# A four-layer graph network on one core: low and high parts split from PSUM, row sums on TensorE, and an earlier start of the masked layer's loads

## The reference, cut to what matters

```python
h = relu(layernorm(x)); x = x + (1 - 0.1 * h - 0.01 * sum(h * (adj @ h), axis=1))          # layer 0
for k in range(2): h = tanh(concat([adj @ h, h]) @ W[k])                                  # layer 1, two hops
mask = (adj != 0); rank = cumsum(mask, axis=1); k = min(deg, 100); pos = rank - (deg - k)
w = mask * where(pos > 0, 0.5 ** (k - pos), 0);  x = x + w @ (h @ weight) + bias           # layer 2, masked
x = x + (tanh(concat([h, t]) @ W1 + b1) @ W2 + b2) + adj @ (h @ B.T) - rowsum(adj) * (h @ B.T)   # layer 3
```

## Time and profile before

| | us |
|---|---|
| median of 3 runs | 698.91 |
| profiled execution, its own time | 700.7 |
| its span, first to last instruction | 698.9 |
| TensorE matmuls busy | 668.3 |
| VectorE busy | 469.6 |
| ScalarE busy | 192.5 |
| GpSimd busy | 114.2 |

### The profile page before, as it was taken

One profiled execution on the slowest core, in us unless ns is written; L12 is line 12 of the kernel. 1 busy time (PEld: TensorE's weight loads), 2 busy tenths in 40 slices (PEclk: granted clock), 3 DMA queues, 4 the chain that ended last, 5 costly groups with the idle time before them and its releaser, 6 DMA issues.

```text
span 698.9 us, 10418 instructions
## 1 busy us (share of the span) xinstructions
PE 668.3 (96%) x3811; PEld 270.2 (39%) x3824; DVE 469.6 (67%) x813; ACT 192.5 (28%) x296; POOL 114.2 (16%) x132
## 2 busy tenths in 40 slices
PE   3999999999999999999999998899999999999997
PEld 1434433334433333333344443444444443333332
DVE  7777767777899999996888888899989810000000
ACT  1101111011111001101111116899998811111111
POOL 4110011110200000001222223222332211211111
PEclk9999999999999999999999999999999999999999
DMA  8999999998589999959999983999999479999992
GB/s 347 422 410 411 413 412 409 418 414 335 190 329 388 420 422 419 415 206 402 384 406 420 419 368 134 362 378 408 414 414 412 191 263 341 417 415 418 417 419 98
DMA packets 42098, 256.51 MB, mean 367 GB/s; under 512 B 5120, under 2 KB 11264, under 8 KB 11840
## 3 DMA queue, kind: packets, MB, share of 16 engines
q1 hardware_dynamic: 38712, 252.85, 89.6%
q10 hardware_dynamic: 3336, 3.00, 1.5%
HBM read 252.28 MB, written 3.54 MB: 366 GB/s over the span
## 4 chain that ended last, share of the span: by engine, by line
PE 53%; DMA 20%; DVE 19%; POOL 4%; issue 3%; ACT 0%; SPq 0%; DVEq 0%; ACTq 0%; POOLq 0%
PE accA L1373 37%; DMA cache<-adj_blocks 10%; DVE uS L1111 8%; DMA land<-adj_blocks 6%; PE accA L1424 4%; PE work L1408 4%; DVE uS L1155 3%; POOL rstd L762 2%; DMA rows_transposed<-rowsT 2%; PE work L1391 1%; PE work L1336 1%; POOL tS L772 1%; PE accA L1342 1%; PE work L1267 1%; PE work L1304 1%
## 5 line engine op out<-in xcount | busy, mean ns | idle before, releaser
L1373 PE MATMUL accA<-land,X 128*64 128x512 f32 x1568 | 374.1, 598 | 13.6 <-DVE X L1197 11.3
L1373 PEld LDWEIGHTS accA<-land,X 128*64 128x64 f32 x1568 | 110.6, 137 | 193.7 <-issue 166.9
L1155 DVE TENSOR_SCALAR uS<-land 128x1024 bf16<-128x1024 f32 (+1 forms) x196 | 134.5, 730 | 30.1 <-DMA land<-adj_blocks 28.4
L1111 DVE TENSOR_TENSOR uS<-uS,land 128x512 f32<-128x512 f32 x178 | 125.2, 704 | 9.6
L1373 PE MATMUL accA<-cache,X 128*64 128x512 f32 x480 | 120.1, 598 | 2.6 <-DMA cache<-adj_blocks 2.6
L591 ACT ACTIVATE wS<-work 128x1024 uint16<-128x1024 f32 x114 | 109.2, 1037 | 8.8 <-PE work L1408 8.7
L769 POOL TENSOR_TENSOR hS<-tS 128x256 f32<-128x256 f32 x24 | 23.5, 978 | 400.5 <-DVE tS L979 400.5
L1097 DVE TENSOR_TENSOR zS<-uS,work 128x256 f32<-128x256 f32 x8 | 3.4, 421 | 123.1 <-PE work L1267 106.9
L1408 PE MATMUL work<-uS,triA 128*128 128x512 bf16 x248 | 74.4, 380 | 2.2 <-DVE uS L1155 1.8
L1424 PE MATMUL accA<-wS,X 128*128 128x512 bf16 x251 | 74.7, 379 | 0.3
L850 ACT ACTIVATE accS<-accA 128x512 f32<-128x512 f32 x32 | 19.1, 598 | 177.3 <-PE accA L1373 165.5
(11 more groups left out here) (109 smaller groups left out, 417.4 us busy)
## 6 DMA issues: line engine op xcount, KB each, us to landing
land<-adj_blocks SPq DMA_DIRECT2D x221, 1024.0 KB, 10.3
cache<-adj_blocks SPq DMA_DIRECT2D x15, 1024.0 KB, 16.7
xin<-x_rows ACTq DMA_DIRECT2D x8, 128.0 KB, 7.6
out_rows<-zS ACTq DMA_DIRECT2D x8, 128.0 KB, 6.9
uS<-counts ACTq DMA_DIRECT2D x60, 4.0 KB
x_rows<-zS SPq DMA_DIRECT2D x7, 128.0 KB, 11.4
rows_transposed<-rowsT SPq DMA_DIRECT2D x7, 128.0 KB, 8.6
wS<-rows_transposed SPq DMA_DIRECT2D x7, 128.0 KB, 8.5
```

Source lines behind the costliest of these rows:

```text
L1111: nc.vector.tensor_tensor(total, total, of[:, i * W:(i + 1) * W], ALU.add)\
L1155: nc.vector.tensor_scalar(masks(p, c, b)[0:rows, :], block_of(p, c, b)[0:rows, :], 0.0, None, ALU.not_equal)\
L1373: last = nc.tensor.matmul(accA[k * D:(k + 1) * D, c % 2, :], tile(X[p % 2], TQ * q + k), of[:, k * W:(k + 1) * W], start=(b == 0), stop=(b ...
```

## The change

- **Stages of L1B** move: join and its copy one block earlier, the row stages too, so that stage 4 has no totals between it and stage 3; norm and turn one block later; the product moves to block 15.
- **High and low parts**: ScalarE writes the high part as float16 straight from PSUM instead of natS; VectorE computes the low part from PSUM and the high part, in the next chunk ("lo", after block 0). GpSimd's `split_rows` goes.
- **Row sums**: the last chunk's totals are not folded; TensorE multiplies them by a column of ones behind the other products, in line after the last block of L1B. Masks 0 to 3 of L2 are made in the last chunk of L1B. The first weigh matmul now waits for `rowsum`, as they share a bank.
- **Order at the seam**: the first triangles come ahead of the last join. The third triangle waits for the low part of chunk 6.
- **SyncE** sends `counts_for(3)` after the first load of the second chunk of L2; the turned rows of L2 and the last chunk's left-over rows are written by ScalarE.
- **L2's join** is done at one place in 16 matmuls of 64 columns; blocks 8 and 13 of its first chunk are made into weights by VectorE.
- **L1A**: stages "added" and "tanh" one block earlier, the left-over stages of L0 two or three.
- **The end** is done in two halves: copy, join, add and write.

```diff
-STAGES_L1A = {1: 2, "added": 4, "tanh": 6, "hop": 8, "hopped": 10}
-STAGES_L2 = {0: 2, "join0": 4, "join1": 5, 4: 5, 5: 7, 6: 10, 7: 13, 8: 15}
-STAGES_L1B = {1: 3, "added": 5, "tanh": 6, 3: 7, 4: 8, 5: 10, "turn": 12, "turned": 13, 6: 14, 8: 15}
+STAGES_L1A = {1: 2, "added": 3, "tanh": 5, "hop": 8, "hopped": 10}
+STAGES_L2 = {0: 2, "join": 4, 4: 5, 5: 7, 6: 10, 7: 13, 8: 15}
+STAGES_L1B = {1: 2, "added": 4, "tanh": 5, 3: 6, 4: 7, 5: 11, "turn": 13, "turned": 14, 6: 15, 8: 15}
...
-         L2: {"tanh": 0, 4: 0, 5: 2, "turn": 8, "turned": 9, 6: 10, 7: 10, 8: 11,
-              "row sums": 14},
+         L2: {"tanh": 0, "join": 1, 5: 1, "turn": 7, "turned": 7, 6: 9, 8: 9, "lo": 9, "left rows": 13},
...
-LEFT_L1A = {"counts": 2, "weights": 3, "left": 5, "left out": 7}
+LEFT_L1A = {"counts": 0, "weights": 1, "left": 2, "left out": 4}
...
                     left_over(1)
-                    counts_for(3)
+                    left_rows_of(sp, NC - 3)
...
                     load(p, c, k)
+                    if (p, c, j) == (L2, 1, 0):
+                        counts_for(3)
...
+                    if p == L2 and c < NC - 1:
+                        act.wait_ge(tr_evac, tr_no(p, c) + 1)
+                        act.dma_start(hT_d[ch(p, c)], rowsT[:, :]).then_inc(hT_out, 16)
                 if at == 8 and p in (L1B, L2):
                     act.wait_ge(nat_done, nat_no(p, c, 1) + 1)
                     if p == L1B:
-                        act.wait_ge(copy_used, copied_no(p, c, 1))
-                        nc.scalar.activation(natS[:, :], nat_of(p, c), ACT.Copy, scale=SCALE).then_inc(nat_evac, 1)
+                        nc.scalar.activation(halves(c, 0), rows4(nat_of(p, c)), ACT.Copy, scale=SCALE).then_inc(hi_rows, 1)
...
+                    if at == "lo":
+                        dve.wait_ge(hi_rows, c + 1)
+                        nc.vector.scalar_tensor_tensor(out=halves(c, D), in0=rows4(nat_of(p, c)), scalar=SCALE, in1=halves(c, 0),
+                                                       op0=ALU.mult, op1=ALU.subtract).then_inc(nat_evac, 1)
...
+                if (p, c) == (L1B, NC - 1) and b in MASKS_AHEAD:
+                    mask(L2, 0, MASKS_AHEAD[b])
...
                 if p == L2 and c == 0:
-                    for b in range(2):
-                        mask(p, c, b)
-                    fold_totals(L1B, NC - 1)
-                    nc.vector.tensor_tensor(part_sums, part_sums, more_sums, ALU.add).then_inc(folded, 1)
                     epilogue("added", before)
-                    for b in range(2, 4):
-                        mask(p, c, b)
+                    dve.wait_ge(sums_done, 1)
+                    nc.vector.tensor_scalar(rowsum[:, :], sums_p, -1.0, None, ALU.mult).then_inc(rowsum_ready, 1)
+                    mask(p, c, 4)
                     epilogue(3, before)
-                    for b in range(4, LEAD):
-                        mask(p, c, b)
+                    mask(p, c, 5)
+                    epilogue(4, before)
...
+            def row_sums():
+
+                pe.wait_ge(folded, SUMMED)
+                pe.wait_ge(totalled, totalled_no(L1B, NC - 1, totals_at(L1B, NC - 1)[-1]))
+                for g in range(4):
+                    for k in range(2):
+                        nc.tensor.matmul(sums_p[g * NT:(g + 1) * NT, :], wt("join", k * NT, (k + 1) * NT),
+                                         part_sums[:, g::4], start=(k == 0), stop=False)
+                for j in range(4):
+                    t = 4 * (NC - 1) + j
+                    last = nc.tensor.matmul(sums_p[:, t:t + 1], totals(NC - 1)[:, j * P:(j + 1) * P], wt("one"),
+                                            start=False, stop=(j == 3))
+                last.then_inc(sums_done, 1)
...
+                if c == 0 and b == 0:
+                    pe.wait_ge(rowsum_ready, 1)
```

More of the change, by code:

```diff
@@ L131 @@
 _at = 0
-for _name, _n in (("hop0", P), ("w1t", 2), ("b1", 2), ("t", 1), ("ident", P), ("join", D), ("full", 1),
+for _name, _n in (("hop0", P), ("w1t", 2), ("b1", 2), ("t", 1), ("ident", P), ("join", D), ("full", 1), ("one", 1),
                   ("hop1", P), ("l2w", P), ("bT", P), ("bias", D), ("w1", 256), ("w2", 2 * D), ("b2", D)):
@@ L341, in last_stages @@
 def last_stages(before):
-    return [(k, before) for k in SUM_STAGES]
+    return [("last " + k, before) for k in SUM_STAGES]
 def sweep_steps(step, finish):
@@ L895, in epilogue @@
                                          bias=hbias[:, h:h + 1]).then_inc(hidden_ready, 1)
+                if at == "last sums":
+                    act.wait_ge(intra_done, c + 1)
+                    act.wait_ge(swept, sweep_no(p, c) + 1)
+                    act.wait_ge(nat_done, nat_no(p, c))
+                    for h in range(2):
+                        nc.scalar.activation(accS[:, h * CH:(h + 1) * CH], accA[:, c % 2, h * CH:(h + 1) * CH], ACT.Copy)\
+                            .then_inc(acc_evac, 1)
+                if at == "last store":
+                    for h in range(2):
+                        act.wait_ge(nat_evac, nat_no(p, c) + 1 + h)
+                        act.dma_start(last_half(chunk(out, ch(p, c)), h), last_half(zS, h)).then_inc(rows_out, 16)
+                if at == "left rows":
+                    left_rows_of(act, c)
                 if at == ("store" if p == L3 else 7) and p in rows_to and not rows_by_sync(p, c):
@@ L1312, in epilogue @@
                     last.then_inc(hop_done, 1)
-                if at == "row sums":
-                    pe.wait_ge(nat_evac, nat_no(L1B, NC - 1, 1) + 1)
-                    pe.wait_ge(folded, SUMMED)
-                    for g in range(4):
-                        for k in range(2):
-                            last = nc.tensor.matmul(sums_p[g * NT:(g + 1) * NT, :], wt("join", k * NT, (k + 1) * NT),
-                                                    part_sums[:, g::4], start=(k == 0), stop=(k == 1))
-                    last.then_inc(sums_done, 1)
                 if at == "stack":
```

146 lines of the change are left out of this document (79 added, 67 removed).

## The result

Before 699.91 us (median of 8 runs), after 695.12 us (693.67 to 697.12, 8 runs): the ratio is 0.9934, 95% interval 0.9918 to 0.9951. The change makes the kernel 4.8 us faster, where 9.2 had been forecast. The profiled execution took 695.5 us with a span of 693.7, for 700.7 and 698.9 before; the 5.2 us between the spans are what follows, stage by stage, from one execution of each kernel.

What follows compares the result with a forecast made beforehand. Two resources were taken as nearly full: TensorE, busy 668 of 699 us, and memory, near 415 GB/s. Terms -3.3 - 3.1 - 1.9 - 0.3 - 0.3 - 0.3 = -9.2 gave 689.7 us against the median 698.9; range 685.5 to 695.5.

Steps and rivals of the forecast that it cites:

- I give half back: Masked layer: memory can't follow TensorE's gain of 3.8 us, so only -1.9 us was kept (bounds -3.8 and +1).
- Second hop, -3.3: Second hop: reordering VectorE's chain shortens the period from 15.66 to 15.17 us, -3.3 us over six periods.
- (c): Second hop: GpSimd's root and scaling are held up by totals beside them; half of -3.3 goes, 691 us; chance 0.04.
- (d): Second hop: memory at 402 GB/s sets every period; only small terms stay, -0.9, 698.0 us; chance 0.06.
- (e): Second hop: VectorE's wait for the high part makes a slower ring, period 17.4 us, in sum +4.2, 703.1 us; chance 0.06.
- First hop, -0.3: First hop: moving the left-over weights up removes TensorE's 0.88 us wait for the tanh; loads take most, leaving -0.3 us.
- Seam, -3.1: Seam from second hop to masked layer: last turn to left-over rows takes 23.4 us against 26.6, -3.1 us.
- Row sums about 0.45: Seam: 12 small matmuls for 8, now in TensorE's line, take about 0.45 us of 3.95 to the first triangle.
- Masked layer, -1.9: Masked layer: shorter joins (-2.2 us) and fewer stalls make -3.8 us for TensorE, of which memory leaves -1.9.
- The sign named for this: Masked layer: joins 15.7 us apart early, then more; VectorE's waits for loads grow from 1.4 us to some 3.
- rival (a): Masked layer: loads take all its gain and a third of the seam's; -6.2 us in sum, 692.7 us; chance 0.20.
- I let the 1.09 us go: Masked layer: TensorE's 1.09 us stall for the late write of transposed rows vanishes once ScalarE issues that write.

Runs made afterwards that it cites:

- e3_evac8_act: The changed kernel with block 8's weights of the masked layer's first chunk made by ScalarE again; 694.61 us, ratio 0.9932.
- e4_sums_halves: The changed kernel with the products of the last totals and the column of ones in two halves of 64 columns; 695.06 us, ratio 0.9944.
- e1_after_half: The changed kernel with the masked layer's 43 loads cut to half their size, so only to find a cause; 691.6 us, ratio 0.9896.
- e6_write_by_sync: The changed kernel with the masked layer's transposed rows written by SyncE again, between its loads; 694.86 us, ratio 0.9943.
- e7_old_join: The changed kernel with the masked layer's old join, two groups of two tiles with 128 columns; 695.98 us, ratio 0.9952.

## Why the prediction was wrong at the seam and in the masked layer

The forecast was 9.2 us and the kernel gained 4.8; 695.12 us lies above 687.5 to 692. Only the second hop came as worked out. Two steps failed: the seam's chain of work, which was to be 3.1 us shorter and was as long as before, and the step "I give half back", which kept 1.9 us of the masked layer where memory took all of it.

*Second hop, -3.3: right, with -3.85.* The mechanism was VectorE's order, and its terms held: the low part at 0.42 us, the totals cover GpSimd. The forecast period was 15.17 us, the measured 15.08, where TensorE's own work (15.1) now sets it. The four totals took 3.23 us, for 1.52 + 1.32 + 0.28. Rivals (c), (d) and (e) fall: beside the totals GpSimd's root and scaling grew to 1.39 and 1.05 us, for 1.01 and 0.61 in the kernel before, as (c) feared, but the totals covered that too and nobody waited for them; memory kept the pace at 15.08 us a chunk; the wait for the high part was 0.28 us.

*First hop, -0.3: not shown.* The profiles have -1.1, but not by the step that was forecast: the stall of the earlier trace rows made way for one of 1.60 us, which was missing in the working, as the weights that were moved up delay ScalarE's copy of `accS`. That the number came out on the right side is chance.

*Seam, -3.1: wrong, 0.0.* Counted as in the working, from the end of block 12, the first triangle comes after 5.30 us, for 3.95; mask 6's 6.44 us later, for 6.7; the left-over rows 14.82 us after that, for 12.1 and the 0.6 allowed for them. The main terms: "Row sums about 0.45" measured 1.4, most of it the four products of the last totals with one column each (eight records with 128 columns of weights, 0.12 us apiece), which I had priced by small matmuls. And the order of VectorE's work was followed only up to mask 6: behind it lie the wait of 0.58 us for hS and the 1.30 us at 437.68 for block 8's weights, which my working never mentions, though the change lists that block among VectorE's. e3_evac8_act and e4_sums_halves show that each of these hid the wait for the left-over rows; only when all three were mended did 2.0 us come out. The 0.6 us for those rows were too little as well: where nothing hides them they cost 1.04 (5.4 us from issue to landing in e3_evac8_act).

*Masked layer, -1.9: wrong, +0.7.* TensorE's part was right: without memory in the way it gained 3.7 us (112.20 to 108.48) for the -3.8 I gave, of it 2.0 from the join (forecast 2.2). The step that failed is "I give half back": memory took all of it and 0.7 more. The first load was 8.3 us earlier and the seventh 6.2, for "some 5.3" and "4 or more", but the lead did not last: in chunks of six loads it is used up at 2.87 - 2.61 = 0.26 us a load, an estimate of 9 us over 36 loads, and against the 90.2 us of e1_after_half it is 13. The rate that a load gets in this layer was in the trace of the kernel before: its seventh and last landing give 2.79 us, above the 2.61 that TensorE's new pace needs. I judged memory by GB/s in slices, in which 414 looked like room. The sign named for this did show: waits for loads grew from 1.4 us, to 5.1 where some 3 were expected. This is rival (a) in its mechanism, with the seam gone too: it gave -6.2, the measured is -4.8.

*The write on ScalarE.* I let the 1.09 us go because ScalarE's transfers of that size had taken 6.9 us; they did (6.7), and the wait of ScalarE is gone. But e6_write_by_sync has the layer at 112.76 and the whole at 694.86 with the write back on SyncE, where it lands 7.9 to 15.2 us after its issue in the first five chunks, so the move gave nothing. The rule of the Trainium skill, "DMA: Bandwidth & Descriptors", section "Issuing engines are not separate DMA queues", is that transfers share the same engines whoever issues them, and only issue time is saved. It held for the total, not for the write's own time to landing, 6.7 us in the median from ScalarE and 9.5 from SyncE.

*Last join and tail.* -0.7 for -0.3, and -0.2 for -0.3. e7_old_join gives the 0.7 back, so it is the join: the old one took 1.03 us with its four tiles in a row, where I had counted twice 0.39, and the new one 0.46, for 0.47. What gave the tail its 0.2 was not tried.

## What to carry to other kernels

Where two resources are nearly full, price each by its own pace in the same unit before summing gains: here one load's landing interval against the time that the faster engine will leave for it. A stall at a seam often hides the next one, so a change that removes one of them should be tried together with the next two in the chain. And count a small transfer that goes as one packet by its full time on one DMA engine (here 0.16 us for 4 KB), not by its share of sixteen. Last, when a stage is moved earlier, look at what now waits behind it: the count weights of the first hop removed a stall of 0.88 us and made one of 1.60.

## What was not expected of the hardware

Sixty transfers of 4 KB cost the loads beside them about 0.12 us each, 0.15 to 0.17 where the queue was long, while the DMA share stood at 1.01 and more; the same counts in eight pieces of 512 bytes cost less (36 loads in 100.9 us for 103.5), and in half the bytes less again (99.2). Time from issue to landing of one 1 MiB load was 4.7 to 5.1 us for the first of the masked layer, with none queued before it, and 15.8 us at 535 us with the queue full, while loads landed 2.9 us apart: so it says how long the queue is, not how fast a load goes. Eight records of one column with 128 columns of weights took 0.98 us from start to start, and sixteen with 64 columns, for the same sums, 0.49: twice as many in half the time. That it is the width of the weights that costs fits this, but alone it would give the same time for both, and no run says what the rest is.
